# Nyström attention on one core: the third softmax's weighted sums of values as f16 halves in place of f32

## What is computed

```python
Q_l = Q.reshape(b, H, M, n // M, HD).mean(axis=-2)
K_l = K.reshape(b, H, M, n // M, HD).mean(axis=-2)
kernel1 = softmax(einsum('bhnd,bhmd->bhnm', Q, K_l))
kernel2 = softmax(einsum('bhmd,bhkd->bhmk', Q_l, K_l))
kernel3 = softmax(einsum('bhmd,bhnd->bhmn', Q_l, K))
SV = (kernel1 @ iterative_inv(kernel2)) @ (kernel3 @ V)
...
h = relu(einsum('btd,edh->ebth', x, Wd1) + bd1)
recon = einsum('ebth,ehd->ebtd', h, Wd2) + bd2
losses = mean((recon - x[None]) ** 2, axis=(2, 3))
idx = argmin(losses, axis=0)
```

## Time and profile before

| | |
|---|---|
| median of 3 runs | 2302.66 us (2300.61 to 2303.02) |
| the profiled execution | 2305.19 us, its span 2303.5 us |
| mean granted TensorE clock | 0.96 of full speed |
| PE / DVE / ACT / POOL busy, share of the span | 87% / 65% / 37% / 29% |
| DMA, mean rate over the span | 65 GB/s |
| one batch in the middle of the run | 135.4 us |

### The profile page before, as it was taken

The page is one execution under the profiler, slowest core; times in us unless marked ns, Lnnn a source line. Parts: engine busy times, 40 slices in busy tenths (PEclk is TensorE's granted clock), DMA queues, the critical chain, the costliest instruction groups (busy, mean ns, idle before and its releaser), DMA issues.

```text
span 2303.5 us, 58849 instructions
## 1 busy us (share of the span) xinstructions
PE 2010.8 (87%) x24985; PEld 1302.1 (57%) x24985; DVE 1504.5 (65%) x3470; ACT 858.9 (37%) x1490; POOL 676.7 (29%) x902
## 2 busy tenths in 40 slices
PE   2588998989899898989989898998989899898945
PEld 2264755647475564747556474755647475564724
DVE  4376667676766767576676757667675767767542
ACT  1243443343344334334443433444343443434321
POOL 2113132331513223151323315132331513233051
PEclk7788999999999999999999999999999999999978
DMA  3323222151422215142221514222151422214020
GB/s 83 82 60 78 44 75 61 26 129 30 115 44 72 59 29 130 29 113 46 74 63 23 130 30 115 44 71 65 25 129 29 115 43 76 63 22 111 11 55 19
DMA packets 232972, 150.71 MB, mean 65 GB/s; under 512 B 153035, under 2 KB 203732, under 8 KB 232693
## 3 DMA queue, kind: packets, MB, share of 16 engines
q1 hardware_dynamic: 232710, 146.95, 27.2%
HBM read 36.98 MB, written 16.78 MB: 23 GB/s over the span
## 4 chain that ended last, share of the span: by engine, by line
PE 57%; DVE 20%; SPq 10%; issue 4%; ACT 3%; POOL 3%; DMA 2%; DVEq 1%; POOLq 0%; ACTq 0%
PE NS L905 11%; SPq L416 10%; PE ringF L1112 9%; PE ringA L1072 5%; PE KV L986 5%; PE ringA L806 4%; PE ringF L1096 4%; PE ringF L1145 3%; DVE stage L1529 2%; DVE mx L1439 2%; DVE mx L1453 2%; PE ringA L948 2%; PE ringA L972 2%; PE ringF L806 2%; PE ringF L1147 2%
## 5 line engine op out<-in xcount | busy, mean ns | idle before, releaser
L1112 PE MATMUL ringF<-x,H 128*128 128x256 f16 x1536 | 237.9, 273 | 0.0
L1453 DVE TENSOR_REDUCE mx<-ringA 128x8 f32<-128x512 f32 x256 | 175.6, 687 | 77.8 <-PE ringA L948 76.7
L651 ACT ACTIVATE E<-ringA,score_scale 128x512 f32<-128x512 f32 x256 | 175.6, 686 | 122.9 <-PE ringA L972 122.9
L806 PE MATMUL ringA<-xT,wqkv 128*128 128x512 f16 x768 | 181.3, 387 | 30.1 <-DMA KS<-KS 13.6
L1112 PE MATMUL ringF<-H 128*128 128x128 f16 x1024 | 204.4, 220 | 1.7 <-DVE H L1542 1.7
L1439 DVE TENSOR_REDUCE mx<-ringA 128x1 f32<-128x512 f32 x256 | 160.3, 684 | 47.1 <-PE ringA L939 46.5
L1096 PE MATMUL ringF<-wd,x2T 128*128 128x512 f16 x768 | 186.7, 382 | 5.0 <-DVE H L1540 3.3
L1506 DVE SCALAR_TENSOR_TENSOR X<-X,NS 128x320 f32<-128x320 f32 x160 | 78.0, 488 | 169.7 <-PE NS L905 164.5
L659 ACT ACTIVATE E<-ringA,score_scale 128x512 f32<-128x512 f32 x256 | 158.8, 685 | 69.9 <-PE ringA L1003 69.9
L469 POOL TENSOR_SCALAR vtmp<-mv,eps_ffn 128x8 f32<-128x8 f32 x16 | 5.1, 316 | 606.9 <-DVE mv L1285 606.9
L469 POOL TENSOR_SCALAR vtmp<-mv,eps_ln 128x8 f32<-128x8 f32 x32 | 9.9, 310 | 552.6 <-DVE mv L1285 544.1
(11 more groups left out here) (250 smaller groups left out, 4330.1 us busy)
## 6 DMA issues: line engine op xcount, KB each, us to landing
KS<-stage SPq DMA_DIRECT2D x384, 64.0 KB, 2.0
QS<-stage SPq DMA_DIRECT2D x384, 64.0 KB, 2.0
xin<-in_L_attn_x_dram SPq DMA_DIRECT2D x16, 1024.0 KB, 11.0
xres<-in_L_attn_x_dram SPq DMA_DIRECT2D x16, 1024.0 KB, 8.1
out_dram<-yout SPq DMA_DIRECT2D x16, 1024.0 KB, 5.5
QS<-LB SPq DMA_DIRECT2D x16, 512.0 KB, 4.4
E<-in_L_attn_w_qkv_dram SPq DMA_DIRECT2D x1, 768.0 KB
E<-in_L_ffn_Wd_dram SPq DMA_DIRECT2D x2, 256.0 KB
```

What stands on the lines that cost most here:

```text
L651: A(E[:, k % ESLOTS, :], ps[:, :], ACT.Exp, scale=score_scale[:, 0:1]).then_inc(freed["s3"].sem, 1)
L806: ins = MM(dst, left(a, k), right(c, k), start=n == 0, stop=n == 3 * KC - 1)
L1112: ins = MM(dst, H[:, a, t, own], src, start=first and i == 0, stop=last and i >= 3, skip_group_check=True)
L1453: V_.reduce_max(mx1[:, t, 8 * h:8 * h + 8], take(b, "m1", k)[:, :].rearrange("p (a m) -> p a m", a=8), AX.X)\
```

## The change

- ACT writes the exponentials of step k twice, into E (f32) and, rounded to f16, into slot k % 4 of a tile E16 that lies in yout's memory. For k = 1, 5, 9, 13 DVE makes the f16 copy instead (`exponentials_hi`), two steps later in its list.
- POOL makes the lower halves (`exponentials_lo`): E minus its f16 value, written as f16, 16 instructions of 128x512 per batch, and from the values two f16 halves and a column of ones (`values16`, six instructions per batch). Both stand ahead of `norm1(b+1)` in POOL's list.
- In `sum_values` the exponentials are now the stationary operand (128 columns) and V16 the moving one: 65 columns for the upper half (values' lower half, upper half, ones), 33 for the lower half. It runs three steps behind the scores in place of two, and waits for POOL. Pairs 0 to 3 accumulate in KV, 4 to 7 in NS[1].
- The result is no longer transposed and its denominators are one column: the 128x256 reciprocal, its product, `values_transpose` and two copies are gone; DVE takes the two banks into SBUF (`values_take`, the first half inside `denominator_maxima`), inverts 128x8 numbers, adds the halves and multiplies.
- `gram` puts the doubled product in 128 columns of its own, and R2 has the factor 2 in its own columns; H's third slot and DVE's doubling (L1542) are gone, and the sum over the bank covers 512 columns in place of 384.
- V lies in E's slots 4 to 7; kernel2's transposes go to NS[0] alone, the denominators to KV. The set-up clears a larger R2, a column of V16, and fills R2 with two more instructions.

```diff
@@ POOL @@
+            def values16(b):
+                for k in range(4):
+                    rows = slice(2 * k, 2 * k + 2)
+                    pool.wait_ge(freed["pv"].sem, freed["pv"].at(b, k + 1))
...
+                    pool.tensor_copy(V16[:, rows, :, HD2:2 * HD2], V[:, rows, :, :]).then_inc(v16.sem, 1)
+                for g in range(2):
+                    rows = slice(4 * g, 4 * g + 4)
...
+                    pool.tensor_tensor(V16[:, rows, :, 0:HD2], V[:, rows, :, :], V16[:, rows, :, HD2:2 * HD2],
+                                       ALU.subtract).then_inc(v16.sem, 1)
+            def exponentials_lo(b):
+                for k in range(16):
+                    if k % 4 == 1:
+                        pool.wait_ge(e_hi.sem, e_hi.at(b, k // 4 + 1))
+                    else:
+                        pool.wait_ge(freed["s3"].sem, freed["s3"].at(b, k + 1))
+                    pool.sem_inc(s_apart, 1)
+                    pool.tensor_tensor(E16[:, k % 4, 1, :], E[:, k % ESLOTS, :], E16[:, k % 4, 0, :], ALU.subtract)\
+                        .then_inc(e_lo.sem, 1)
@@ ACT, exp3 @@
+                if k % 4 != 1:
...
+                    A(E16[:, k % 4, 0, :], ps[:, :], ACT.Exp, scale=score_scale[:, 0:1])
@@ PE, sum_values @@
-                pe.wait_ge(freed["s3"].sem, freed["s3"].at(b, k + 1))
+                pe.wait_ge(e_lo.sem, e_lo.at(b, k + 1))
...
-                        ins = MM(KV[32 * j:32 * j + 32, (2 * g + i) * P:(2 * g + i + 1) * P], onesf[:, :] if i else V[:, t, p, :],
-                                 E[:, k % ESLOTS, j * P:(j + 1) * P], start=t == 0 and i == 0, stop=t == T - 1,
-                                 skip_group_check=True)
+                    MM(acc_bank[:, j * VW:(j + 1) * VW], E16[:, k % 4, 0, cols], V16[:, t, p, 0:VW], start=t == 0 and j == 0,
+                       stop=False, skip_group_check=True)
+                    ins = MM(acc_bank[:, j * VW + HD2:(j + 1) * VW], E16[:, k % 4, 1, cols], V16[:, t, p, HD2:VW], start=False,
+                             stop=t == T - 1, skip_group_check=True)
@@ PE, body @@
-                    if k >= 2:
-                        sum_values(b, k - 2)
+                    if k >= 3:
+                        sum_values(b, k - 3)
...
+                sum_values(b, 13)
+                if ffn_too:
+                    gram(b - 1, 0, range(0, T // 2))
                 for k in range(14, 16):
                     sum_values(b, k)
-                if ffn_too:
-                    gram(b - 1, 0, range(0, T // 2))
-                values_transpose(b)
                 fold1_transpose(b)
@@ DVE @@
+            def exponentials_hi(b, k):
+                dve.wait_ge(freed["s3"].sem, freed["s3"].at(b, k + 1))
+                if k >= 4:
+                    dve.wait_ge(kv_full.sem, kv_full.at(b, k - 4 + 1))
+                V_.tensor_copy(E16[:, k % 4, 0, :], E[:, k % ESLOTS, :]).then_inc(e_hi.sem, 1)
...
-                V_.tensor_scalar(H[:, 2, t, :], H[:, 0, t, :], 2.0, None, ALU.mult).then_inc(h2.sem, 1)
...
+                    if k % 4 == 3:
+                        exponentials_hi(b, k - 2)
-                values_normalise(b)
                 fold1_rows(b)
+                values_take(b, 1)
                 values_place(b)
```

More of the change, by code:

```diff
@@ L59, in sandwich_kernel @@
     GP = P // HD2
-    GR = P + C
+    GR = P + C + P
     ESLOTS = 8
     SHIFT = 1.0
+    VW = 2 * HD2 + 1
+    DM = 272
     ctx = ExitStack()
@@ L137, in sandwich_kernel @@
         st2 = sb("st2", [P, 4, PAIRS])
+        rden = sb("rden", [P, PAIRS])
+        vsum = sb("vsum", [P, PAIRS, D])
+        kvs = sb("kvs", [P, PAIRS, VW])
         K2c = sb("K2c", [P, PAIRS, M])
@@ L515, in attn_residual @@
                     ins.then_inc(ao_done.sem, 1)
+            def values16(b):
[3 more added lines that the diff above has]
+                    pool.sem_inc(s_apart, 1)
+                    if k == 0 and not first(b):
+                        pool.wait_ge(kv_full.sem, kv_full.at(b - 1, 2 * T))
+                        pool.sem_inc(s_apart, 1)
+                    pool.tensor_copy(V16[:, rows, :, HD2:2 * HD2], V[:, rows, :, :]).then_inc(v16.sem, 1)
+                for g in range(2):
+                    rows = slice(4 * g, 4 * g + 4)
+                    pool.wait_ge(v16.sem, v16.at(b, 4 + g))
+                    pool.sem_inc(s_apart, 1)
+                    pool.tensor_tensor(V16[:, rows, :, 0:HD2], V[:, rows, :, :], V16[:, rows, :, HD2:2 * HD2],
[6 more added lines that the diff above has]
+                        pool.wait_ge(freed["s3"].sem, freed["s3"].at(b, k + 1))
+                    pool.sem_inc(s_apart, 1)
+                    pool.tensor_tensor(E16[:, k % 4, 1, :], E[:, k % ESLOTS, :], E16[:, k % 4, 0, :], ALU.subtract)\
+                        .then_inc(e_lo.sem, 1)
             def norm2(b):
@@ L542, in body @@
                     norm2(b - 1)
+                values16(b)
+                exponentials_lo(b)
                 if more:
@@ L564, in _ @@
             step(pool.memset(hid[64:65, :], 1.0))
+            step(pool.memset(V16[:, :, :, 2 * HD2:2 * HD2 + 2], 1.0))
             step(pool.memset(sel32[:, :], 0.0))
@@ L649, in exp3 @@
                 if k >= ESLOTS:
-                    act.wait_ge(kv_full.sem, kv_full.at(b, k - ESLOTS + 1))
+                    act.wait_ge(e_lo.sem, e_lo.at(b, k - ESLOTS + 1))
+                elif k == 4:
+                    act.wait_ge(v16.sem, v16.at(b, 6))
+                if k % 4 != 1:
+                    if k >= 4:
+                        act.wait_ge(kv_full.sem, kv_full.at(b, k - 4 + 1))
+                    elif k == 0 and not first(b):
+                        act.wait_ge(x2lo.sem, x2lo.at(b - 1, 2))
+                    A(E16[:, k % 4, 0, :], ps[:, :], ACT.Exp, scale=score_scale[:, 0:1])
                 A(E[:, k % ESLOTS, :], ps[:, :], ACT.Exp, scale=score_scale[:, 0:1]).then_inc(freed["s3"].sem, 1)
@@ L913, in kernel2_transpose @@
                     for i in range(4):
-                        ins = halves(NS[1 - q][:, i * M:(i + 1) * M], K2c,
+                        ins = halves(NS[0][:, (4 * q + i) * M:(4 * q + i + 1) * M], K2c,
                                      lambda r, e, p: identf[r, e * M:(e + 1) * M], 4 * q + i)
@@ L1351, in _ @@
                                  hid_sc[rows, 0:1], None, ALU.mult)
+                V_.tensor_scalar(R2[rows, :, P + C + e * HID:P + C + (e + 1) * HID],
+                                 ringF[0][rows, :].rearrange("p (q n) -> p q n", q=EP)[:, :, e * HID:(e + 1) * HID],
+                                 hid_sc[rows, 0:1], 2.0, ALU.mult, ALU.mult)
                 for q in range(EP):
@@ L1431, in first_iterate @@
                 dve.wait_ge(cb_full.sem, cb_full.at(b, 1))
-                V_.reciprocal(cinv[:, :], NS[1][:, 256:256 + PAIRS]).then_inc(dm.sem, 1)
+                V_.reciprocal(cinv[:, :], KV[:, DM + P:DM + P + PAIRS]).then_inc(dm.sem, 1)
                 dve.wait_ge(dm.sem, dm.at(b, 4))
```

74 lines of the change are left out of this document (38 added, 36 removed).

## The result

The changed kernel takes 2496.56 us (median of 4 runs, 2486.28 to 2501.53) against 2302.84 for the kernel before: 1.0833 times as long, 95% interval 1.0808 to 1.0857. It is slower, as forecast, but by 194 us where 50 were forecast, far outside the range.

What follows compares the result with a forecast made beforehand. The prediction took a DVE-PE chain to bound the loop, with new waits at POOL setting the pace. Waits (46 us), longer sums (2) and set-up (1.6) added 50 us to a median of 2302.7: about 2352, range 2285 to 2388.

Steps and rivals of the forecast that it cites:

- What bounds the kernel: In a batch's loop: a chain changing between DVE (22.1 us of work) and PE; freeing banks faster gains at most 4.5 us.
- What is removed: PE's sums fall from 0.57 to 0.24 us, 5.3 us per batch; DVE loses H's doublings (1.0 us in loop) and the reciprocal.
- What is added: DVE casts (0.43 us) and copy (0.4), ACT 12 exponentials (8.2), hidden; POOL 16 subtractions at 1.15 us, below the loop's length.
- The new waits: PE's sums of k = 1, 5, 9, 13 wait for cast and POOL: +2.2 us in the loop, +0.7 at its end.
- hand schedule: The loop laid out from earlier durations: DVE 22.6 us busy and 6.2 idle, 28.8 in all, then 6.9 to Newton and Schulz.
- a clock below 1.00: In the loop: listed as a sign that the forecast is wrong, since PE would stand idle longer than now; no size given.
- The values' halves (about 8 us) fit ahead of the loop: POOL's work on the values, about 8 us a batch, finds room ahead of the loop; no cost was added for it.
- The rival of the disturbance: POOL and DVE disturb each other; a third of the loop's subtractions at twice 1.15 us, 2 us more a batch: 2384, chance 0.22.
- The sum: Whole run: 16 x (2.2 + 0.7) = 46, 15 x 0.14 = 2, set-up 1.6; +50 us, about 2352.
- the rival at 2265: DVE is the bound and the waits vanish: -3.0 us in the loop, +0.5 at its end per batch; chance 0.18.
- The lower bound of 0.8 us for a subtraction: POOL's 128x512 subtraction at its fastest, in proportion to a one-input instruction of 0.55 us for 256 columns.
- the 2319: Total time in us if subtractions took 0.8 us: the waits at POOL shrink by 2.1 us a batch.

Runs made afterwards that it cites:

- e8: Changed kernel with POOL's values subtractions late, all f16 copies on ACT, and no lower halves of the exponentials (f16 accuracy alone): 2238.24 us, ratio 0.9719.
- e7: Changed kernel, values' subtractions late, all f16 copies on ACT, sum_of_squares behind values_place, 24 filling matmuls in steps 3, 10, 11: 2278.15 us, ratio 0.9882.
- e4: Kernel before with the Gram product's part of the change alone: 2302.23 us, ratio 0.9986.
- e2: Changed kernel with ACT making all 16 f16 copies of the exponentials, DVE's four casts gone: 2379.50 us, ratio 1.0335.
- e5: Changed kernel with 208 useless matmuls a batch filling PE's idle time ahead of four waits: 2415.84 us, ratio 1.0482.
- e1: Changed kernel with POOL's two subtractions for the values' lower halves held back until behind fold3_rows: 2429.76 us, ratio 1.0537.
- e9: Changed kernel with DVE's four casts one step earlier in its list: 2413.52 us, ratio 1.0484.

## Why the prediction was wrong, step by step

- *What bounds the kernel*, a chain that changes between DVE and PE in the loop: it fits the runs. PE's shorter sums shorten the loop only where ACT and POOL leave them room: by 2.1 us in e8, and next to nothing in e7.
- *What is removed*: 0.24 us per sum taken; eight matmuls from 1425.03 to 1425.26, 0.23 us, at full clock. The estimate from the Trainium skill's load time (0.43, "TensorE: Matmul & The Clock Gate", LDWEIGHTS) did not hold; the row that the prediction took in its place did. The Gram part took 1.0 us of DVE's work out of the hand-made loop; alone it brings 0.4 us there, 0.1% of the time (e4).
- *What is added*: POOL's subtraction 1.15 us taken, 1.16 measured; DVE's cast 0.43 taken, 0.41 measured; the copy 0.4 and 0.42. ACT stayed hidden (e2 with four more exponentials is faster).
- *The new waits*: right in place and in sum. With the clock held (e5) the loop and its end take 36.6 us; the hand schedule had 0.42 + 28.8 + 6.9 = 36.1, that is +2.9 on before, and 3.4 were measured. The single waits were less well met: behind POOL PE waits 1.9, 0.9, 1.2 and 2.0 us, where 1 to 2 us each were said, with the longest ahead of `first_iterate` and of the last sums.
- *What failed first* is a term that is missing from the sum: each wait of PE was priced at its length, and what PE did behind it at the durations of the earlier trace rows, that is at clock 1.00. Behind the waits of 3.0 and 1.9 us PE worked at 0.50 for 3.4 us each, and behind one of 1.4, which 1.2 and 2.0 followed, for 17 us. It cost 4.5 us a batch in the loop and its end and 1.2 ahead of it, 5.7; e5 gets back 5.0. The text named a clock below 1.00 only as a thing that would prove it wrong, and gave it no price and no chance; that sign came true (0.79 in the loop). The trace of the kernel before held the price, in the maxima of the third softmax ahead of the loop:

```profile
1293.56 0.99 PE L939 MATMUL ringA<-KS,QlB 96*128 96x512 f16 x3 [3.69 <-DVE stage L1388]
...
1295.35 2.67 PE L806 MATMUL ringA<-wqkv,xT 128*128 128x256 f16 x12
1297.86 0.60 PE L939 MATMUL ringA<-KS,QlB 96*128 96x512 f16 x2
...
1299.62 1.48 PE L806 MATMUL ringA<-wqkv,xT 128*128 128x256 f16 x12 [0.21 <-DVE mx L1439]
1300.94 0.60 PE L939 MATMUL ringA<-KS,QlB 96*128 96x512 f16 x2
```

Behind a wait of 3.7 us twelve matmuls take 2.51 us from start to start, and the same twelve 1.32 a little later.
- *What failed second* is the sentence "The values' halves (about 8 us) fit ahead of the loop". They fit POOL's time, but they lie beside DVE's fold3_rows, on which PE waits. Their block costs 2.6 us a batch directly (with the clock 3.8; e1 gets back 4.2).
- *The rival of the disturbance* had the right mechanism in the wrong place. It looked at the subtractions slowing down in the loop; they did not (1.16 us). DVE's small operations did. With the Trainium skill's rule ("SBUF — State Buffer", Who interferes with whom: a POOL operation that got the port pair first holds it for its whole length, and a DVE operation with two inputs in SBUF, or a cast in one of the two-port modes, waits until then) the traces agree: 1.51 and 2.02 us, ending with POOL's. The forecast used the rule for the new casts alone and did not go through DVE's list for old instructions that it now catches.
- *The sum*: 2.9 per batch became 11.6, of which 2.6 are the block, 3.4 the waits and 5.7 the clock (rounded). The range ended at 2388, just above the one rival that was slower than the sum (2384), and no bound let a second effect follow from the same wait. At its other end it left out the rival at 2265, which had a chance of 0.18. The lower bound of 0.8 us for a subtraction, and with it the 2319, is wrongly worked out: 0.55 us for 256 columns is 1.1 for 512 in proportion.

## What to carry to other kernels

When a change makes PE wait in a stretch where it was hardly ever idle, price the work behind the wait at both levels of the clock, and put the difference in the sum or in the range; a run with idle time filled by useless matmuls tells the two apart for little work. When work moves to POOL, list every DVE instruction that reads two operands or casts in SBUF in the same stretch, above all small ones on a chain that others wait for, and move POOL's work to a place where there are none. When one engine hands over every fourth item of a queue that another works off in order, the items behind it wait too, so its place in the first engine's list matters more than its own length (e9).

## What the hardware showed that I had not expected

- In the changed kernel the clock of PE fell from 1.00 to 0.50 behind waits of 1.4 to 3.0 us and stayed there for 3.4 to 17 us. The length of a wait alone did not settle it: behind the same wait of 3.0 to 3.3 us ahead of fold3_transpose the clock fell in 15 of 15 batches of the changed kernel, but stayed at 1.00 up to the loop in 4 of 15 in e2 and in 7 of 15 in e9 (the first batch left out). What else decides is open. 208 useless matmuls a batch make the kernel 81 us faster.
- A DVE operation on 8 columns took up to 2.0 us beside a POOL subtraction of 1024 columns, while POOL's own duration did not change (2.07 us on average there and 2.07 in e1, where the two lie apart). The maxima read from PSUM were not held up (0.69 us at most).
- POOL casts 128x512 from f32 to f16 in 0.62 us, half of what its subtraction of the same size takes (1.16).
